# Attention scores in blocks of 32 keys: four matmuls of 32 columns where one of 125 stood

## The chip, the cores and the metric

The kernel runs on one NeuronCore of one Trainium2 chip; the other seven cores are idle. The core has engines with instruction streams of their own: PE (TensorE, matrix multiply; PEld is its weight load), ACT (ScalarE), DVE (VectorE), POOL (GpSimd) and SP, which here only issues DMAs. They meet through semaphores. The metric is device time in microseconds (us) of one execution, and less is better. The kernel before takes 2458.41 us (median of three runs, 2457.47 to 2459.47).

## The reference

The input is 8 waveforms of 120000 samples. Each is cut into 1500 frames of 80 samples, and then (biases and shapes cut):

```python
h = einsum('bfr,hr->bfh', x, W) + b          # 8 x 1500 x 256
h = gelu(layernorm(h) * ln_gamma + ln_beta)
n = layernorm(h)                             # 16 heads of 16 columns each
scores = einsum('bhqd,bhkd->bhqk', Q, K) / 4 # Q, K, V from n
attn = softmax(scores, axis=-1)              # 1500 x 1500 for each head and batch
h = h + einsum('bhqk,bhkd->bhqd', attn, V) @ Wo.T + bo
h = h + ffn(layernorm(h))
```

In the last line each of 16 experts takes 8 // 16 = 0 tokens of an axis of 8, so that `ffn` comes down to a layernorm with a scale and an offset per column. Nearly all the work is in the scores and their softmax: 8 x 16 x 1500 x 1500 exponentials, 288 million.

## The kernel before

**Tiling.** A batch is one waveform. Its 1500 tokens are 12 tiles of 125 (`T`), or 3 chunks of 500 (`QC`). Its 16 heads are 4 groups of 4. A unit is one group of heads and one chunk of 500 queries; there are 12 units in a batch and 96 in the kernel. A unit takes all 1500 keys. An item is one head and one tile of 125 keys against the 500 queries: a score block of 125 x 500. A unit has 48 items, done in 8 rounds of 6, so the kernel has 96 x 8 = 768 rounds and 4608 items.

**Score matmuls.** Queries and keys are kept as two halves of 16 bits each, so that one head has 64 rows (`KR`) to sum over. Even heads lie on partitions 0 to 63, odd heads on 64 to 127. One item is one matmul on line 829: 64 rows, 125 columns of weights (the keys), 500 moving columns (the queries). Items come in pairs, an even and an odd head, and `scores(n, first, 2, ...)` issues one pair: it fills two of PSUM's banks 0 to 5, and only its last matmul raises the semaphore `s_sc`.

**The round.** Program order on PE in a round is: pair one (banks 4 and 5), pair two (banks 0 and 1), pair three (banks 2 and 3), then the attends, then the pieces beside. Each pair first waits (`s_ex`) until ACT has emptied the banks it writes. ACT has three exponentials in a round, each over 2 banks (125 x 1000): line 486 for banks 0 and 1, line 489 for banks 2 and 3, line 494 for banks 4 and 5. So pair one of a round feeds line 494 of the same round, while pairs two and three feed lines 486 and 489 of the next. The three pairs of banks are all the buffering there is between the two engines.

**Attends.** `attend` (line 853) multiplies the exponentials of one tile of keys with V: four program matmuls, one for each head, each 125 rows by 32 columns of weights and 500 moving columns in f32. Every f32 matmul is two in the trace, so one attend is 8 there. Even rounds have one attend and odd rounds two; the second of an odd round waits for line 494 of its own round. The results gather in bank 6 or 7, and a column of ones in V gives the softmax's sums.

**Pieces.** Work of the next batch, and the output of the last, is cut into pieces (`tok`, `turn`, `qk`, `val`, `norm`, `flag`, `out`), placed by the table `PLAN` into rounds, usually one a round. Their matmuls (lines 774, 790, 799, 819, 806) already work in blocks of 32 columns, made by `blocks(n)`; `turn` (line 783) transposes with 128 columns. The table is the same in both kernels. Once a batch, in unit 2, ACT leaves the exponentials for a GELU.

**The second pass.** `exact_max` is a path with exact row maxima that runs only if a bound on the scores fails. It doesn't run on this input.

Of the kernel before, what the change touches and what calls it, by code (L numbers as in the profile page):

```python
# [5 lines left out]
def audio_tower(nc, x, tok_wT, tok_b, tok_g, tok_be, wqT, bq, wkT, bk, wvT, bv, woT, bo, ln_g, ln_b, out):  # L6
# [5 lines left out]
    NT, T = x.shape[2], x.shape[3]  # L12
# [3 lines left out]
    QC = 500  # L16
# [121 lines left out]
    with ExitStack() as ctx:  # L138
        def sb(name, shape, dt=f32):
            return ctx.enter_context(nc.sbuf_tensor(name, shape, dt))  # L140

        ident = sb("ident", [128, 128])
        ones = sb("ones", [128, 128])
# [17 lines left out]
        QA = sb("QA", [128, 2, 2, S], f16)  # L161
        KA = sb("KA", [128, 2, 2, S], f16)
# [8 lines left out]
        diag = sb("diag", [T, HG, QC])  # L171
# [15 lines left out]
        PS = ctx.enter_context(nc.psum_tensor("PS", [128, 8, 512], f32))  # L187
# [577 lines left out]
        def _(pe):  # L765

            def blocks(n):
                return [(lo, min(lo + 32, n)) for lo in range(0, n, 32)]
# [54 lines left out]
            def scores(n, first, count, exact_max):  # L823
                g, c = (n % NU) // NC, n % NC
                G = n // NC
                for m in range(first, first + count):
                    t, h, bank = m // HG, m % HG, m % 6
                    rows = slice(64 * (h % 2), 64 * (h % 2) + 64)
                    last = pe.matmul(PS[0:T, bank, 0:QC], KA[rows, G % 2, h // 2, t * T:(t + 1) * T],  # L829
                                     QA[rows, G % 2, h // 2, c * QC:(c + 1) * QC], start=True, stop=not exact_max)  # L830
                    if exact_max:
                        last = pe.matmul(PS[0:T, bank, 0:QC], ones[0:T, 0:T], diag[:, h, :], start=False, stop=True)
                last.then_inc(s_sc, 1)

            def row_scores(n):
# [43 lines left out]
            def unit(b, u, exact_max):  # L879
                n = b * NU + u  # L880
                R0, bank, used = PER * n, 7 - n % 2, UNIT_USES[n]
                if exact_max or n == 0:
                    if u % NC == 0:
                        pe.wait_ge(s_ld, at(s_ld, 64 * (n // NC + 1)))
                    if n > 0:
                        pe.wait_ge(s_ex, at(s_ex, 3 * R0))
                    if exact_max:
                        row_scores(n)
                    scores(n, 0, 2, exact_max)
                    scores(n, 2, 2, exact_max)  # L890
                for r in range(PER):
                    R = R0 + r
                    if R > 0:
                        pe.wait_ge(s_ex, at(s_ex, 3 * R))
                    scores(n, 6 * r + 4, 2, exact_max)
                    pe.wait_ge(s_ex, at(s_ex, 3 * R + 1))
                    if r == PER - 1 and not exact_max and n + 1 < B * NU and (u + 1) % NC == 0:
                        pe.wait_ge(s_ld, at(s_ld, 64 * ((n + 1) // NC + 1)))
                    for j in range(2):
                        if j:  # L900
                            pe.wait_ge(s_ex, at(s_ex, 3 * R + 2))
                        if r < PER - 1:
                            scores(n, 6 * r + 6 + 2 * j, 2, exact_max)
                        elif not exact_max and n + 1 < B * NU:
                            scores(n + 1, 2 * j, 2, False)
                    q = r // 2
                    if r == 0:
                        pe.wait_ge(s_free, at(s_free, used))
                        if n > 1:
                            pe.wait_ge(s_ov, at(s_ov, n - 1))  # L910
                    if r % 2 == 0:
                        attend(n, 3 * q)
                    else:
                        attend(n, 3 * q + 1)
                        pe.wait_ge(s_ex, at(s_ex, 3 * R + 3))
                        attend(n, 3 * q + 2)
                    used = beside(b, u, r, bank, used)
# [86 lines left out]
```

## Time and profile before

| | |
|---|---|
| time, median of 3 | 2458.41 us |
| profiled execution, its own time | 2458.36 us |
| its span, first to last instruction | 2456.6 us |
| mean granted TensorE clock, share of 2.4 GHz | 0.971 |
| PE busy, matmuls | 2237.6 us, 19500 |
| ACT busy | 2155.3 us, 2332 instructions |
| DVE busy | 920.3 us |
| POOL busy | 371.5 us |
| DMA | 133.62 MB, 54 GB/s |

A busy share adds up the time in which at least one instruction of the engine is under way. Matmuls overlap, and the profile models their ends, so what matters for PE is the time from the start of one matmul to the start of the next. The exponentials on ACT overlap as well: each is on the books for about 1.01 us while the next starts 0.88 to 0.90 us after it.

### The profile page before, as it was taken

How to read it: one execution, taken by the hardware profiler on the slowest of the kernel's cores; microseconds unless marked ns; L12 is line 12 of the kernel's file. 1: busy time of each engine (PE TensorE's matmuls, PEld its weight loads, DVE VectorE, ACT ScalarE, POOL GpSimd, SP SyncE). 2: the span in 40 equal slices, each digit the busy share in tenths (PEclk: the TensorE clock that was granted, in tenths of full speed). 3: DMA queues.
4: the chain of work that ended last, by engine and by line, in shares of the span. 5: the costliest groups of instructions: out<-in, count | busy, mean ns of one | idle time of the engine just before them, and what ended most of it. 6: DMA issues, size and time to landing. Idle time of an engine off the chain costs nothing.

```text
span 2456.6 us, 47924 instructions
## 1 busy us (share of the span) xinstructions
PE 2237.6 (91%) x19500; PEld 669.8 (27%) x19500; DVE 920.3 (37%) x2075; ACT 2155.3 (88%) x2332; POOL 371.5 (15%) x495
## 2 busy tenths in 40 slices
PE   4589999999999999999999999999999999998892
PEld 1222223222232223222232222322222222222221
DVE  7442235432354334532345233542335332330114
ACT  0098999989999899998999899998999989999991
POOL 2211102211021111210112110211112110110002
PEclk7799999999999999999999999999999999999996
DMA  2311221222112222212212221222222122111101
GB/s 71 107 37 40 66 67 41 57 66 65 50 40 66 64 66 49 57 48 58 74 40 52 70 66 40 50 62 60 69 54 50 41 65 67 47 44 39 33 6 32
DMA packets 109922, 133.62 MB, mean 54 GB/s; under 512 B 32263, under 2 KB 89670, under 8 KB 109694
## 3 DMA queue, kind: packets, MB, share of 16 engines
q1 hardware_dynamic: 107158, 128.64, 20.8%
q8 instruction: 156, 2.56, 0.4%
q10 hardware_dynamic: 2536, 1.83, 0.3%
q14 instruction: 72, 0.59, 0.1%
HBM read 55.16 MB, written 61.44 MB: 47 GB/s over the span
## 4 chain that ended last, share of the span: by engine, by line
issue 47%; PE 27%; ACT 10%; POOL 8%; DVE 3%; POOLq 1%; DMA 1%; SPq 1%; DVEq 0%; ACTq 0%
PE PS L853 12%; PE PS L829 8%; PE PS L790 5%; ACT prob L489 4%; ACT prob L486 4%; POOL sq L380 2%; POOL Y L388 2%; ACT prob L494 2%; POOL rs L390 2%; POOLq L389 1%; PE PS L799 1%; PE PS L774 1%; DVE z L550 1%; DVE HL L568 1%; POOL rs L367 1%
## 5 line engine op out<-in xcount | busy, mean ns | idle before, releaser
L853 PE MATMUL PS<-prob,Vst 125*32 125x500 f32 x9216 | 1131.4, 593 | 0.2 <-ACT prob L489 0.2
L494 ACT ACTIVATE prob<-PS 125x1000 f32<-125x1000 f32 x768 | 776.4, 1011 | 135.9 <-PE PS L829 134.6
L829 PE MATMUL PS<-QA,KA 64*125 64x500 f16 x4608 | 769.0, 406 | 84.5 <-ACT prob L489 45.7
L486 ACT ACTIVATE prob<-PS 125x1000 f32<-125x1000 f32 x768 | 775.3, 1010 | 80.4 <-PE PS L829 80.3
L489 ACT ACTIVATE prob<-PS 125x1000 f32<-125x1000 f32 x768 | 784.4, 1021 | 0.0
L829 PEld LDWEIGHTS PS<-QA,KA 64*125 64x125 f16 x4608 | 255.9, 131 | 861.6 <-ACT prob L486 413.6
L853 PEld LDWEIGHTS PS<-prob,Vst 125*32 125x32 f32 x9216 | 219.6, 108 | 424.6 <-issue 242.5
L566 DVE TENSOR_SCALAR HL<-PS,b_qk 128x500 f16<-128x500 f32 x96 | 70.9, 739 | 504.1 <-PE PS L790 427.7
L790 PE MATMUL PS<-zT,w_qk 128*32 128x500 f32 x1536 | 197.4, 596 | 8.9 <-DVE Osb L611 7.6
L380 POOL TENSOR_TENSOR sq<-HL 128x2000 bf16<-128x2000 f16 x24 | 84.5, 3522 | 752.4 <-DVE HL L568 752.4
L611 DVE COPY Osb<-PS 128x500 f32<-128x500 f32 x96 | 65.0, 677 | 257.5 <-PE PS L853 257.5
L819 PE MATMUL PS<-w_o,oT 128*32 128x256 f32 (+1 forms) x1536 | 102.5, 388 | 36.7 <-DMA oT<-On 22.2
L799 PE MATMUL PS<-w_v,zT 128*32 128x256 f32 (+1 forms) x1536 | 104.2, 394 | 21.6 <-DVE Vst L573 20.9
L385 POOL TENSOR_SCALAR rs<-mv 125x1 f32<-125x1 f32 x96 | 26.1, 272 | 595.6 <-DVE mv L633 595.0
L623 DVE TENSOR_TENSOR On<-Den,Osb 128x500 f32<-128x500 f32 x96 | 103.7, 1080 | 7.9 <-issue 0.9
L629 DVE TENSOR_TENSOR Hs<-Hs,PS 125x256 f32<-125x256 f32 x96 | 39.6, 412 | 166.4 <-PE PS L819 166.4
L790 PEld LDWEIGHTS PS<-zT,w_qk 128*32 128x32 f32 x1536 | 48.1, 113 | 129.9 <-issue 100.8
L819 PEld LDWEIGHTS PS<-w_o,oT 128*32 128x32 f32 (+1 forms) x1536 | 46.2, 111 | 113.3 <-issue 36.2
L642 DVE SCALAR_TENSOR_TENSOR Y<-Hs,rs,Y 125x256 f32<-125x256 f32 x96 | 73.2, 763 | 7.2
L517 DVE BATCH_NORM_STATS2 st<-PS 125x6 f32<-125x256 f32 x96 | 36.5, 422 | 102.8 <-PE PS L774 102.8
L799 PEld LDWEIGHTS PS<-w_v,zT 128*32 128x32 f32 (+1 forms) x1536 | 47.2, 111 | 99.3 <-issue 38.7
L568 DVE SCALAR_TENSOR_TENSOR HL<-PS,b_qk,HL 128x500 f16<-128x500 f32 x96 | 70.9, 739 | 7.9 <-issue 0.9
(79 smaller groups left out, 955.0 us busy)
## 6 DMA issues: line engine op xcount, KB each, us to landing
qk_halves_scratch<-HL SPq DMA_DIRECT2D x384, 125.0 KB
QA<-qk_halves_scratch SPq DMA_DIRECT2D x64, 375.0 KB, 5.0
KA<-qk_halves_scratch SPq DMA_DIRECT2D x64, 375.0 KB, 7.2
oT<-On SPq DMA_DIRECT2D x384, 31.2 KB, 2.0
out<-Y SPq DMA_DIRECT2D x24, 500.0 KB
X<-in_x SPq DMA_DIRECT2D x8, 468.8 KB, 7.9
thin<-Osb SPq DMA_DIRECT2D x96, 7.8 KB
Den<-thin SPq DMA_DIRECT2D x96, 7.8 KB
```

Of the source, the lines that this page charges most:

```text
L380: pool.tensor_tensor(sq[:, :, :], HL[:, :, 0, :], HL[:, :, 0, :], ALU.mult).then_inc(s_sq, 1)
L486: act.activation(prob[0:T, 6 * p:6 * p + 2, :], PS[0:T, 0:2, 0:QC], ACT.Exp, scale=scl)\
L489: act.activation(prob[0:T, 6 * p + 2:6 * p + 4, :], PS[0:T, 2:4, 0:QC], ACT.Exp, scale=scl)\
L494: act.activation(prob[0:T, 6 * p + 4:6 * p + 6, :], PS[0:T, 4:6, 0:QC], ACT.Exp, scale=scl)\
L568: dve.scalar_tensor_tensor(out=HL[:, i % 4, 1, :], in0=PS[:, bank, 0:QC], scalar=bias, in1=HL[:, i % 4, 0, :], op0=ALU.add, op1=ALU.subtra ...
L623: dve.tensor_tensor(On[:, :], Den[:, :], Osb[:, :], ALU.mult).then_inc(s_on, 1)
L642: dve.scalar_tensor_tensor(out=y, in0=h, scalar=rs3[:, n % 2:n % 2 + 1], in1=y, op0=ALU.mult, op1=ALU.add).then_inc(s_y, 1)
L790: ins = pe.matmul(PS[lo:hi, bank, 0:QC], w_qk[:, c, w, m * 128 + lo:m * 128 + hi], zT[:, c, :], start=(c == 0), stop=(c == KC - 1))
L799: last = pe.matmul(PS[lo:hi, bank, 0:D], zT[:, c, t + lo:t + hi], w_v[:, c, :], start=(c == 0), stop=(c == KC - 1))
L819: last = pe.matmul(PS[lo:hi, bank, 0:D], oT[:, m, e * T + lo:e * T + hi], w_o[:, m, :], start=(m == 0), stop=(m == KC - 1))
L829: last = pe.matmul(PS[0:T, bank, 0:QC], KA[rows, G % 2, h // 2, t * T:(t + 1) * T], QA[rows, G % 2, h // 2, c * QC:(c + 1) * QC], start=Tr ...
L853: last = pe.matmul(PS[lo:lo + 2 * HD, 6 + n % 2, 0:QC], Vst[:, b % 2, t, g * HG + j, :], prob[0:T, (HG * t + j) % 12, :], start=(t == 0), ...
```

## The change

Where an item was one matmul with 125 columns of weights, it is four: blocks of 32, 32, 32 and 29 keys. Each block writes its own 32 partitions of the same PSUM bank, and all four read the same 500 queries. The same is done in the path that doesn't run here. The pair's last matmul, which raises the semaphore, is now the fourth block of the odd head. `blocks` is the helper that the other matmuls use already.

```python
def blocks(n):
    return [(lo, min(lo + 32, n)) for lo in range(0, n, 32)]
```

```diff
                     t, h, bank = m // HG, m % HG, m % 6
                     rows = slice(64 * (h % 2), 64 * (h % 2) + 64)
-                    last = pe.matmul(PS[0:T, bank, 0:QC], KA[rows, G % 2, h // 2, t * T:(t + 1) * T],
-                                     QA[rows, G % 2, h // 2, c * QC:(c + 1) * QC], start=True, stop=not exact_max)
+                    for lo, hi in blocks(T):
+                        last = pe.matmul(PS[lo:hi, bank, 0:QC], KA[rows, G % 2, h // 2, t * T + lo:t * T + hi],
+                                         QA[rows, G % 2, h // 2, c * QC:(c + 1) * QC], start=True, stop=not exact_max)
                     if exact_max:
-                        last = pe.matmul(PS[0:T, bank, 0:QC], ones[0:T, 0:T], diag[:, h, :], start=False, stop=True)
+                        for lo, hi in blocks(T):
+                            last = pe.matmul(PS[lo:hi, bank, 0:QC], ones[0:T, lo:hi], diag[:, h, :],
+                                             start=False, stop=True)
                 last.then_inc(s_sc, 1)
```

On PE, in the middle of a batch, the end of an odd round and a whole even round with a `qk` piece read like this before (QA and KA are queries and keys, prob the exponentials, Vst is V, zT and w_qk belong to the piece):

```order
L853 MATMUL PS<-prob,Vst 32x500 x8
L790 MATMUL PS<-zT,w_qk 32x500 x4
L829 MATMUL PS<-QA,KA 125x500 x6
L853 MATMUL PS<-prob,Vst 32x500 x4
L790 MATMUL PS<-zT,w_qk 32x500 x4
```

The same even round, from its second item on, is this in the changed kernel:

```order
L830 MATMUL PS<-QA,KA 32x500 x3
L830 MATMUL PS<-QA,KA 29x500
L830 MATMUL PS<-QA,KA 32x500 x3
L830 MATMUL PS<-QA,KA 29x500
L830 MATMUL PS<-QA,KA 32x500 x3
L830 MATMUL PS<-QA,KA 29x500
L830 MATMUL PS<-QA,KA 32x500 x3
L830 MATMUL PS<-QA,KA 29x500
L830 MATMUL PS<-QA,KA 32x500 x3
L830 MATMUL PS<-QA,KA 29x500
L856 MATMUL PS<-prob,Vst 32x500 x4
L790 MATMUL PS<-zT,w_qk 32x500 x4
```

Six matmuls have become 24, and nothing has moved past anything else: the order of pairs, attends and pieces is unchanged, and so are all other engines.

## Rows read from the trace of the kernel before

**Rows 1.** The page: busy time and instructions, and the clock in 40 slices.
```profile
PE 2237.6 (91%) x19500; PEld 669.8 (27%) x19500; DVE 920.3 (37%) x2075; ACT 2155.3 (88%) x2332; POOL 371.5 (15%) x495
...
PEclk7799999999999999999999999999999999999996
...
q8 instruction: 156, 2.56, 0.4%
```

**Rows 2.** Waits of ACT and PE, 130 to 2290 us: total us, times, longest.
```profile
ACT prob L494 <- PE PS L829: 132.3, 160, 4.1
...
PE PS L829 <- ACT prob L489: 37.5, 95, 0.5
```

**Rows 3.** Timeline of ACT, 1204.4 to 1211: start us, us, what it ran.
```profile
1204.51 1.01 ACT L489 ACTIVATE prob<-PS 125x1000 f32<-125x1000 f32 x1
...
1206.30 1.02 ACT L486 ACTIVATE prob<-PS 125x1000 f32<-125x1000 f32 x1
1207.18 1.03 ACT L489 ACTIVATE prob<-PS 125x1000 f32<-125x1000 f32 x1
1208.21 1.00 ACT L494 ACTIVATE prob<-PS 125x1000 f32<-125x1000 f32 x1
...
1210.00 1.01 ACT L489 ACTIVATE prob<-PS 125x1000 f32<-125x1000 f32 x1
```

**Rows 4.** Timeline of PE from 1202.26: one row for each group of matmuls.
```profile
1202.26 0.92 PE L829 MATMUL PS<-QA,KA 64*125 64x500 f16 x6
...
1205.93 1.04 PE L853 MATMUL PS<-prob,Vst 125*32 125x500 f32 x8
1206.79 1.02 PE L790 MATMUL PS<-zT,w_qk 128*32 128x500 f32 x8
1207.75 0.94 PE L829 MATMUL PS<-QA,KA 64*125 64x500 f16 x6
```

**Rows 5.** Timeline of PE in windows under 0.1 us: pairs and sets of four.
```profile
1202.26 0.42 PE L829 MATMUL PS<-QA,KA 64*125 64x500 f16 x2
1202.52 0.66 PE L829 MATMUL PS<-QA,KA 64*125 64x500 f16 x4
1205.58 0.42 PE L829 MATMUL PS<-QA,KA 64*125 64x500 f16 x2
1205.93 0.63 PE L853 MATMUL PS<-prob,Vst 125*32 125x500 f32 x4
1206.37 0.60 PE L853 MATMUL PS<-prob,Vst 125*32 125x500 f32 x4
...
1204.40 0.60 PE L853 MATMUL PS<-prob,Vst 125*32 125x500 f32 x4
1204.93 0.42 PE L829 MATMUL PS<-QA,KA 64*125 64x500 f16 x2
```

**Rows 6.** Durations of lines 829, 853 and 806: ns, least, median and most.
```profile
L829 PEld LDWEIGHTS PS<-QA,KA x4608: 128/129/228, 116.3 to 2401.4; 64*125 64x125 f16 x192
L829 PE MATMUL PS<-QA,KA x4608: 368/421/675, 116.4 to 2401.4; 64*125 64x500 f16 x192
...
L853 PE MATMUL PS<-prob,Vst x9216: 579/582/1041, 119.6 to 2403.4; 125*32 125x500 f32 x197
...
L806 PEld LDWEIGHTS PS<-sq,head_sel x96: 92/97/102, 67.1 to 2097.2; 128*32 128x32 bf16 x96
L806 PE MATMUL PS<-sq,head_sel x96: 371/376/600, 67.1 to 2097.6; 128*32 128x500 bf16 x96
```

**Rows 7.** Timeline of PE: one norm piece after a wait, four matmuls of 16 bits.
```profile
100.72 0.40 PE L806 MATMUL PS<-sq,head_sel 128*32 128x500 bf16 x4 [2.15 <-POOL sq L380]
```

**Rows 8.** Timeline of PE: the last transpose of a turn, and the pair behind it.
```profile
1183.12 0.48 PE L783 MATMUL PS<-ident,z 125*128 125x125 f32 x3
1183.33 0.27 PE L783 MATMUL PS<-ident,z 125*128 125x125 f32 x1
...
1183.53 0.43 PE L829 MATMUL PS<-QA,KA 64*125 64x500 f16 x2
```

## The prediction, made before the changed kernel ran

> **What bounds the kernel now.** I read the page's busy shares first, then the waits, then short timelines of ACT and PE side by side. PE is busy for 91% of the span and ACT for 88% [rows 1]: two engines near full, so the question is how they are tied. In the waits, PE waits for ACT in some places (pair three for line 489) and ACT for PE in others (line 494 for a pair) [rows 2]. Neither is simply the bound; they take turns in a loop.
>
> The timelines show the loop. Exponentials start 0.88 to 0.90 us apart, except at 1208.21, which comes 1.03 us after the one at 1207.18 [rows 3]: ACT stood about 0.14 us. Follow that back. Line 494 at 1208.21 needed pair one, which started at 1207.75, so 0.46 us from a pair's start to its exponential. Pair one stood behind a `qk` piece (1206.79), and that behind an attend (1205.93) [rows 4]. The attend stood behind pair three at 1205.58 [rows 5], and pair three had waited for the exponential of line 489 that ran from 1204.51 to 1205.52 [rows 3]. The chain from one line 489 to the line 494 four places on is
>
> 1.07 (exponential and its signal) + 0.35 (pair three to attend) + 0.86 (attend) + 0.96 (piece) + 0.46 (pair one to line 494) = 3.70 us,
>
> where ACT alone would need 4 x 0.885 = 3.54 us. From line 494 the next line 489 follows two places on, 1.79 us later (1208.21 to 1210.00), and the loop closes: 3.70 + 1.79 = 5.49 us for two rounds. The PE rows say the same: pair one at 1202.26 and at 1207.75, 5.49 us apart [rows 4]. ACT's floor for two rounds is 6 x 0.885 = 5.31 us. Where pieces are heavier, PE never waits and its own sum is the period. So in both regimes a nanosecond on PE's path between pairs and attends counts, down to ACT's floor, and 384 such double rounds make the kernel. What lies outside (start, the GELU once a batch, the end) has no part in the change.
>
> **The change, part by part.** 4608 score matmuls become 18432, and as many weight loads. All that counts is what one pair costs PE: two matmuls before, eight now.
>
> *Streaming.* A matmul occupies its part of the array for its 500 moving columns. Two matmuls of a pair, on the two halves of the rows, start together: two end within 0.42 us, and the median of a single one is 421 ns [rows 5, 6]. The second pair starts at 1202.52, 0.26 us after the first, and the third joins within 0.24 us [rows 5]. Four matmuls of 32 columns side by side also start together: four of line 806 take 0.40 us in all, where one has 371 to 376 ns [rows 6, 7]. So neither splitting rows in two nor columns in four costs streaming time. No row shows both splits at once. Bounds: eight start together (0 added), or the two heads go one after the other (0.21 us added to a pair: 500 columns at 2.4 GHz). I take 0, since both splits alone are free.
>
> The Trainium skill, "TensorEngine Tiling (Array Packing)", Tiling Modes, lists 64 rows by 32 columns as a mode with eight tiles that load and multiply independently; no row here has that mode, so this is only cited.
>
> *Weight load.* The first pair after a wait, or behind a change of shape, can't load ahead. Its matmuls show 421 ns against a least of 368 [rows 6], and its distance to the next is 0.26 where 0.21 would be the stream: 0.05 us of load laid open for 125 columns. The load instruction itself is 129 ns for 125 columns and 97 for 32 [rows 6], so 32 ns less; scaled by the columns, 0.052 x 32/125 leaves 13 ns open, so 39 less. I take a gain of 37 ns for each open load. Bounds: 0 (the loads of eight blocks queue up) and 52.
>
> *Spread.* Eight matmuls don't start in the same instant. Four of 16 bits take 0.40 us, of which one has 376 ns and the open load 13 [rows 6, 7]: some 11 ns for three steps, 3 to 4 ns each. Two score matmuls take 0.42, where one has 421 ns [rows 5, 6]: a few ns at most. Sets of f32 spread wider, 0.60 for four with a median of 582 ns [rows 5, 6], 18 to 20 ns for three steps. At 3.3 ns a step eight matmuls spread over 23 ns, 20 more than a pair now; at 6.7 ns, the pace of f32, 47, so 44 more. I take 3.3, as the operands have 16 bits. The pair's signal and the switch to the attends wait for the last.
>
> *The switch of shape.* From the last set of an attend to the next pair takes 0.53 us (1204.40 to 1204.93), where set to set takes 0.44 with an open load (1205.93 to 1206.37) [rows 5] and 0.42 without (1206.37 to 1206.79) [rows 4, 5]. So 0.09 us beyond spread and stream. It isn't only the columns: from the last transpose, with 128 columns and all rows, to a pair, with 125 columns and 64 rows, takes 0.20 us (1183.33 to 1183.53), where transposes follow at 0.11 (three take 0.48, one 0.27) [rows 8]. A change of rows alone costs about as much. In the changed kernel pairs and attends share the column shape and still differ in rows (64 and 125), so I keep 0.09 at both ends of the scores.
>
> The Trainium skill, "TensorEngine Tiling (Array Packing)", Key Properties, says that changing the tiling mode drains the engine. By that rule the switch stays, and the trace agrees with its 0.09 us.
>
> *Issue and instruction fetch.* PE gets 27648 more instructions beside 39000. Its instructions come in 156 packets, 2.56 MB in the whole run, 0.4% of the DMA engines [rows 1]; 1.77 MB more is nothing to 133 MB. I cost it at nothing; if PE's queue ran dry it would show as issue gaps of up to about a microsecond at each of some 110 more packets, 110 us at worst.
>
> *The sum.* Each chain passes two pairs with open loads (pair three, pair one) and two spreads: 2 x (-37 + 20) = -34 ns. A round in which PE never waits has one open load and one spread before the attends: -37 + 20 = -17, and two of them -34. Either way 34 ns for a double round, and 5.49 - 0.034 = 5.456 stays above ACT's 5.31. 384 x 0.034 = 13 us. Some rounds have slack or wait for DVE, which a faster PE doesn't help; I take off a tenth. Forecast: 2458.36 - 12 = 2446.4 us for the profiled execution, which is within 0.1 us of the median (2458.41), so 2446. Its own range goes from both loads at -52 with the small spread (384 x 2 x 0.032 = 25, 2434) to a load gain of 25 (2455).
>
> **Rivals.**
>
> *The spread eats the load.* With the pace of f32, 2 x (-37 + 44) = +14 ns a double round: 384 x 0.014 = +5 us, 2464. With no gain in the load and the small spread, 2 x 20: +15 us, 2474. With both against it, 2 x 44: +34 us, 2492. For it: f32 sets do spread so [rows 5], and eight loads have to pass seven waiting matmuls where four pass three. Against it: four matmuls of 16 bits spread less [rows 7]. It ends on the slower side when the spread of a pair grows by more than its open load shrinks, 37 ns. In the middle it is no change.
>
> *The two heads take turns.* If eight can't run at once, a pair takes 0.42 us instead of 0.21. Each chain has two pairs: 2 x 0.21 - 0.034 = +0.39 us, 148 us, 2606. With pair two in the way as well, where PE never waits, 6 x 0.21 = 1.26 a double round, 480 us, 2940. For it: no row has both splits. Against it: each is free alone.
>
> *The switch falls away.* If only the column shape drained the array, four switches of 0.09 us would go: 0.36 for a double round, of which ACT's floor leaves 5.49 - 5.31 = 0.18 in the light rounds. 384 x 0.18 = 69 us, 2390. For it: attends and pieces with 32 columns follow one another at the stream's pace (1205.93 to 1206.79 for two sets [rows 4]). Against it: rows 8.
>
> *Issue.* If the sequencer can't hand out the 16 instructions of a pair as fast as the four of today, the spread grows. With as much for each step as four matmuls have in all, 24 ns (0.40 less 0.376 [rows 6, 7]), eight spread over 7 x 24 = 168, 165 more than now: 2 x (165 - 37) = +0.26 us a double round, 98 us, 2556. Against it: those four start within that time together. The Trainium skill, "TensorE: Matmul & The Clock Gate", in Part 1, gives a floor of about 25 ns from start to start of small matmuls; across the parts of the array the trace contradicts it [rows 7].
>
> **Chances.** The forecast 0.54. The spread eats the load 0.28, most of it between 2454 and 2480. The heads take turns 0.04, the switch falls away 0.07, issue or fetch 0.07. A measurement can tell 0.2%, 5 us, so "same" is 2453.5 to 2463.3. Faster: 0.50 of the forecast's 0.54 and the 0.07, 0.57. Same: the rest of it, 0.04, and 0.14 of the second case, 0.18. Slower: 0.25. The range 2430 to 2482 holds the forecast and most of the second case and leaves out the last three.
>
> **What the profile after would show.** Line 830 with 18432 matmuls, in sets of eight that start within 25 ns. Open loads: the common matmul behind a wait some 13 ns above the least, where it is 53 now. Pair three to attend 0.34 us, attend to pair one unchanged at 0.53. Double rounds of 5.45 to 5.46 us. ACT's idle time before line 494 some 12 us below the 132.3 of rows 2, each exponential still about 1.01 us. The clock keeps its 9s. Wrong would be: sets of four 0.2 us apart (heads take turns), a pair to exponential time above 0.46 (spread), 0.44 from attend to pair (no switch), or gaps with no releaser on PE (fetch).

## The result, and the profile after

The changed kernel takes 2454.66 us (median of 20 runs) against 2457.69 for the kernel before: ratio 0.9985, with a 95% interval of 0.9978 to 0.9992. One run of each kernel was far slower (4097 and 11536 us), and the ratio is taken without them. That is 3 to 4 us faster, where 12 were forecast. The sign held, and so did the chain that the forecast followed, but not the size: two thirds of the gain are missing.

The page of the changed kernel, beside [rows 1]:

```profile
span 2453.0 us, 75572 instructions
PE 2220.3 (91%) x33324; PEld 613.4 (25%) x33324; DVE 920.1 (38%) x2075; ACT 2153.5 (88%) x2332; POOL 370.5 (15%) x495
...
PEclk7799999999999999999999999999999999999996
...
q8 instruction: 264, 4.33, 0.7%
```

13824 matmuls more, and PE's busy time is 17 us less. A busy time that adds up modelled lengths says little here. ACT's waits for PE between 130 and 2290 us, beside [rows 2]:

```profile
ACT prob L494 <- PE PS L830: 129.7, 153, 4.1
```

132.3 before, so 2.6 us less, which is about what the total shows. Durations of line 830, beside [rows 6]:

```profile
L830 PEld LDWEIGHTS PS<-QA,KA x18432: 87/89/148, 116.3 to 2397.7; 64*32 64x32 f16 x150, 64*29 64x29 f16 x49
L830 PE MATMUL PS<-QA,KA x18432: 367/382/622, 116.3 to 2397.7; 64*32 64x500 f16 x152, 64*29 64x500 f16 x47
```

The common matmul fell from 421 ns to 382. Above the least of its row that is 53 ns before and 15 now, the load that lies open: the load term as forecast. Now one chain in short windows of the timeline (start, length, what, how many): pair three, the attend behind it, then pair one and line 494, which stood waiting for it:

```profile
1081.74 0.40 PE L830 MATMUL PS<-QA,KA 64*32 64x500 f16 x8
1082.07 0.63 PE L856 MATMUL PS<-prob,Vst 125*32 125x500 f32 x4
...
1083.89 0.40 PE L830 MATMUL PS<-QA,KA 64*32 64x500 f16 x8
1083.33 1.04 ACT L489 ACTIVATE prob<-PS 125x1000 f32<-125x1000 f32 x1
1084.36 1.00 ACT L494 ACTIVATE prob<-PS 125x1000 f32<-125x1000 f32 x1
```

All eight matmuls of a pair lie within 0.40 us: the two splits together cost no streaming. Pair three to attend is 0.33 us, 0.35 before [rows 4, 5], as forecast. But pair one to line 494 is 0.47 to 0.48 us, 0.46 to 0.47 before [rows 3, 4], where the forecast's 17 ns less would be 0.45, and more than 0.46 was to be a sign of being wrong. The rows round these to 10 ns; the medians over all rounds, from the trace's start times in ns, are the two distances on which everything below rests:

| median, ns | before | changed |
|---|---|---|
| first to last matmul of a pair | 3 | 23 |
| pair one to pair two, its load open | 262 | 222 |
| **pair three to attend** | 354 | 334 |
| **pair one to line 494**, where ACT waited | 467 | 477 |
| the second bold row less the first: what only ACT's start sees | 113 | 143 |
| pair one to the rise of its semaphore, where ACT waited | 444 | 455 |
| two rounds | 5511 | 5503 |

The spread of 23 ns and the load gain of 40 are the forecast's to a few ns. The signal to ACT is 30 ns later beyond both. The trace also holds the moment at which `s_sc` rises (the last row but one). ACT starts 22 or 23 ns behind it in both kernels, so the lateness is in the semaphore's rise and not in ACT.

### The profile page after: what moved, and what is told of

The parts are those of the page before. It is cut to its first block, busy times and chain, and to the rows that moved or that the text cites. A ratio compares the mean times of both kernels' runs of the same rounds, so it can differ in the third digit from the quotient of the medians.

```text
span 2453.0 us, 75572 instructions
## 1 busy us (share of the span) xinstructions
PE 2220.3 (91%) x33324; PEld 613.4 (25%) x33324; DVE 920.1 (38%) x2075; ACT 2153.5 (88%) x2332; POOL 370.5 (15%) x495
## 4 chain that ended last, share of the span: by engine, by line
issue 49%; PE 21%; ACT 14%; POOL 8%; DVE 3%; DMA 2%; POOLq 1%; SPq 1%; DVEq 0%; ACTq 0%
PE PS L856 9%; ACT prob L489 6%; PE PS L830 6%; ACT prob L486 5%; PE PS L790 4%; POOL sq L380 2%; POOL Y L388 2%; ACT prob L494 2%; POOL rs L390 2%; DMA qk_halves_scratch<-HL 1%; SPq L246 1%; DVE HL L568 1%; DVE HL L566 1%; POOLq L389 1%; DVE z L550 1%
## 5 line engine op out<-in xcount | busy, mean ns | idle before, releaser
L830 PE MATMUL PS<-QA,KA 64*32 64x500 f16 (+1 forms) x18432 | 751.9, 381 | 97.5 <-ACT prob L489 48.8
L830 PEld LDWEIGHTS PS<-QA,KA 64*32 64x32 f16 (+1 forms) x18432 | 200.5, 90 | 907.3 <-ACT prob L486 416.2
L573 DVE TENSOR_TENSOR Vst<-PS,b_v 125x256 f32<-125x256 f32 x96 | 40.1, 421 | 88.5 <-PE PS L799 88.5
```

Source lines behind the costliest of these rows:

```text
L830: last = pe.matmul(PS[lo:hi, bank, 0:QC], KA[rows, G % 2, h // 2, t * T + lo:t * T + hi], QA[rows, G % 2, h // 2, c * QC:(c + 1) * QC], st ...
```

## The experiments

The theory after the trace, called the tail below: the semaphore that starts ACT is raised about 5 ns later for each matmul that ends with the last one. Its rival: the double rounds are bound by something else, and the chain's nanoseconds don't count. A narrower one: the lateness belongs to the shape with 32 columns, not to the number.

### Blocks of 64 keys

```diff
-                    for lo, hi in blocks(T):
+                    for lo, hi in ((0, 64), (64, T)):
```

> Blocks of 64 and 61 keys: four matmuls for each pair instead of two (before) or eight (changed). Tail theory: the signal of a pair comes about 4.8 ns later for each further matmul that ends with it, beside the spread of the starts (3.3 ns each) and less the open load saved (25 ns for 61 columns). From a pair's first matmul to line 494: 467 - 25 + 7 + 10 = 459 ns (467 before, 477 changed). Pair three to attend: 354 - 25 + 7 = 336 ns. Together -26 ns a double round, 384 times: 10 us below the kernel before, about 2448. Rival, the open load never reached the signal and the spread does by half: 470 ns and 336 ns, -15 ns, about 2452. Rival, the light double rounds are bound by something other than this chain: about 2455 as with the changed kernel.

Measured: 2448.14 us (5 runs) against 2458.12, ratio 0.9959 (0.9945 to 0.9972). The two distances are 457 and 334 ns, 459 and 336 expected by the tail. The same chain in this kernel:

```profile
1075.71 0.41 PE L830 MATMUL PS<-QA,KA 64*64 64x500 f16 x4
1076.04 0.63 PE L856 MATMUL PS<-prob,Vst 125*32 125x500 f32 x4
...
1077.86 0.41 PE L830 MATMUL PS<-QA,KA 64*64 64x500 f16 x4
1078.32 1.00 ACT L494 ACTIVATE prob<-PS 125x1000 f32<-125x1000 f32 x1
```

Pair three to attend is the same 0.33 us as with blocks of 32 (less load gained, less spread paid), and pair one to line 494 is 0.46. Here 30 ns of a chain are saved instead of 10, and the time falls by 10 us instead of 3.7 (0.0041 and 0.0015 of 2458). That rejects the rival that other things bind the light rounds. It is also the kernel that beats both: the intervals of the two ratios don't overlap, though the two kernels were not measured side by side.

### Blocks in pairs two and three, or in pair one alone

```diff
-                    for lo, hi in blocks(T):
+                    for lo, hi in (((0, T),) if m // 2 % 3 == 2 else blocks(T)):
```

(the other kernel has the two choices exchanged)

> Pair one of each round whole (125 columns), pairs two and three in blocks of 32; so the column shape changes between pair one and pair two at the same 64 rows. Tail theory and additive chain: pair one to line 494 back at 467 ns, pair three to attend 334 ns, so the short waits of ACT before line 494 go from 156 ns (before) and 151 (changed) to about 136. Pair one to pair two takes 262 before and 223 changed; if a change of columns alone drains, it takes about 0.31 us here. Where PE never waits that costs some 40 to 50 ns a round, hidden in rounds in which pair three waits for ACT. Total 2450 to 2458. Rival, bound elsewhere: short waits stay at 151 to 156. Rival, a change of columns alone doesn't drain: 0.21 to 0.26 us from pair one to two and a total near 2450.

Measured: 2456.07 us (11 runs), ratio 0.9998 (0.9989 to 1.0007): no change. Pair one to line 494 is back at 466 ns. Pair one to pair two takes 355 ns instead of 262, so a change of columns alone, at the same 64 rows, costs 93 ns:

```profile
1205.35 0.42 PE L830 MATMUL PS<-QA,KA 64*125 64x500 f16 x2
1205.70 0.60 PE L830 MATMUL PS<-QA,KA 64*32 64x500 f16 x13
```

The second row starts 0.35 us after the first (it holds pair two and the start of pair three, since the window cuts it). Behind the turns of unit 3, where the whole wait of two rounds falls on one exponential, ACT's wait went from 156 ns to 136, as expected: the 20 ns of pair three arrive whole. In most other rounds pair three now starts late behind the extra switch of shape, since its own wait for ACT is too short to cover it, and the waits are divided otherwise (141 and none before, 77 and 40 in unit 9). The total stands still because gains and losses meet. A batch has 48 double rounds; taken from line 494 to line 494 (medians over the six middle batches), 32 of these places are 20 ns faster, but six are 25 to 48 ns slower, one is 192 slower, and one, of which more below, 234.

> The other way round: pair one in blocks of 32, pairs two and three whole. Tail theory: pair one to line 494 477 ns, pair three to attend 354, short waits of ACT 156 + 10 = 166 ns, and a switch more in each round where PE never waits: 2460 to 2468. Rival, bound elsewhere: short waits at 151 to 156 and a total near 2457.

Measured: 2465.85 us (6 runs), ratio 1.0033 (1.0021 to 1.0045), within what was expected. Pair one to line 494 477 ns, as in the changed kernel, so the lateness goes with the pair that is in blocks: the semaphore rises 454 ns after pair one's start here, and 444 in the kernel with blocks in pairs two and three. The wait behind the turns is 174 and not 166: the switch isn't wholly hidden, which the expectation had wrong.

### The same matmuls cut along the queries

```diff
-                    last = pe.matmul(PS[0:T, bank, 0:QC], KA[rows, G % 2, h // 2, t * T:(t + 1) * T],
-                                     QA[rows, G % 2, h // 2, c * QC:(c + 1) * QC], start=True, stop=not exact_max)
+                    for q0, q1 in ((0, QC // 2), (QC // 2, QC)):
+                        last = pe.matmul(PS[0:T, bank, q0:q1], KA[rows, G % 2, h // 2, t * T:(t + 1) * T],
+                                         QA[rows, G % 2, h // 2, c * QC + q0:c * QC + q1],
+                                         start=True, stop=not exact_max)
```

> Whole 125 keys, the 500 queries of each item in two matmuls of 250: four matmuls for each pair, of which only two end together. Tail theory by matmuls that end together: pair one to line 494 467 + 3 to 5 ns, short waits 160, total 1 to 3 us above the kernel before. Rival, the tail is by the number of instructions since the last signal: 467 + 10 + 5 = 482 ns, total about +6 us. If loading the same weights again is not hidden under 104 ns of stream, pair to pair grows by about 50 ns and the total by 20 us or more.

Measured: 2462.37 us (11 runs), ratio 1.0017 (1.0007 to 1.0026).

```profile
1083.00 0.43 PE L830 MATMUL PS<-QA,KA 64*125 64x250 f16 x4
1083.36 0.63 PE L854 MATMUL PS<-prob,Vst 125*32 125x500 f32 x4
...
1085.18 0.33 PE L830 MATMUL PS<-QA,KA 64*125 64x250 f16 x2
1085.66 1.00 ACT L494 ACTIVATE prob<-PS 125x1000 f32<-125x1000 f32 x1
```

Pair three to attend is 362 ns, 8 more than before, and pair one to line 494 479, 12 more. The second is closer to the count of instructions (482) than to the count of those that end together (470 to 472). But most of it is seen by the attends too, so it is PE that is longer: the two heads now start 7 ns apart instead of 3. Of the tail proper, the difference of the two, 113 has become 117: 4 ns for two more instructions of which none ends together with the last pair, against 10 in the blocks of 64. So the number of instructions alone doesn't explain it, but a rest of 4 ns stays unexplained.

### Fewer matmuls in the same shape

Three kernels, one run each. The first leaves out the fourth block of every item, the second the odd heads with blocks of 32, the third the odd heads of the kernel before; their outputs lack those scores.

```diff
-                    for lo, hi in blocks(T):
+                    for lo, hi in blocks(T)[:3]:
```

```diff
+                    if h % 2:
+                        continue
                     rows = slice(64 * (h % 2), 64 * (h % 2) + 64)
```

> The changed kernel with the fourth block of every item (keys 96 to 124 of each tile) left out, so its scores aren't computed: six matmuls of 32 columns end together instead of eight. By the number of matmuls that end together (5 ns each): pair one to line 494 477 - 7 (spread) - 10 = 460 ns, pair three to attend 327 ns, the difference of the two 133 (143 with eight, 123 with four of 64, 113 with two). If the later signal belongs to the mode with 32 columns and not to the number: 470 ns, difference 143.

> The changed kernel with the odd heads' scores left out: four matmuls of 32 columns, on one half of the rows. By the number: pair one to line 494 477 - 13 - 20 = 444 ns, pair three to attend 321, difference 123. By the mode: 464 ns, difference 143.

> The kernel before with the odd heads' scores left out: one matmul of 125 columns for each pair. By the number: pair one to line 494 467 - 3 - 5 = 459 ns, pair three to attend 351, difference 108. If the signal's lateness isn't by the number of matmuls: 464 ns, difference 113.

Pair one and line 494 in the same round of each, six, four and one matmuls (the line numbers are those of each kernel):

```profile
1080.03 0.40 PE L830 MATMUL PS<-QA,KA 64*32 64x500 f16 x6
1080.48 1.00 ACT L494 ACTIVATE prob<-PS 125x1000 f32<-125x1000 f32 x1
```

```profile
1088.58 0.39 PE L832 MATMUL PS<-QA,KA 64*32 64x500 f16 x4
1089.03 1.00 ACT L494 ACTIVATE prob<-PS 125x1000 f32<-125x1000 f32 x1
```

```profile
1096.42 0.42 PE L831 MATMUL PS<-QA,KA 64*125 64x500 f16 x1
1096.88 1.00 ACT L494 ACTIVATE prob<-PS 125x1000 f32<-125x1000 f32 x1
```

0.45, 0.45 and 0.46 us from row to row. All kernels together, medians in ns:

| matmuls that end together | columns | pair one to line 494 | pair three to attend | difference |
|---|---|---|---|---|
| 1 (one head) | 125 | 458 | 351 | 107 |
| 2 (before) | 125 | 467 | 354 | 113 |
| 4 (one head) | 32 | 444 | 321 | 123 |
| 4 (blocks of 64) | 64 | 457 | 334 | 123 |
| 6 | 32 | 460 | 329 | 131 |
| 8 (changed) | 32 | 477 | 334 | 143 |

The difference rises by 5 ns a matmul, and two kernels with four have the same 123 with 32 columns on one half of the rows and 64 columns on both. So it is the number, not the shape. The semaphore's rise says the same without the attends: it comes 14, 19, 30, 30, 39 and 50 ns after the modelled end of the pair's last matmul (the rows of the table in order; 24 in the halves), and ACT starts 22 or 23 ns after the rise in every one of the kernels. The Trainium skill, "TensorE: Matmul & The Clock Gate", Why this matters for your kernels, has a fit of this kind for the tail of a set of tiles, with 4.7 ns for each tile; the slope here is (143 - 107) / 7 = 5.1, and the trace agrees.

The whole times of these three (2445.59, 2459.68 and 2486.26 us in one run each, against 2459.97) don't follow their chains in the last two. The mean granted clock was 0.962 in both (0.973 in the run of the kernel before beside them), and ACT's wait in the round behind the GELU grew from 0.2 us to between 1.6 and 2.4 in each batch after the first. That the lighter load of PE is why the clock was lower is not shown. They serve for the distances alone.

## Why the prediction was wrong

**What bounds the kernel: right.** The loop through pair three, attends, pair one and ACT was the right one. 20 ns off (blocks in pairs two and three) and 20 on (halves) moved the wait behind the turns of unit 3 from 156 ns to 136 and to 177, and 30 off (blocks of 64) to 128. Weighed with 384 double rounds, -10, -30 and +20 ns give -3.8, -11.5 and +7.7 us, against ratios that stand for -3.7, -10.1 and +4.2. The last is only half, and that isn't slack in the chain. Of the 48 double rounds of a batch, from line 494 to line 494, 41 are within 5 ns of -10 in the changed kernel, 39 within 5 ns of -30 with blocks of 64, and 39 within 5 ns of +20 in the halves, heavy ones among them.

What hides the rest is the clock. In unit 4 of every batch but the last, PE stands 3 us for DVE's `Vst`, and towards the end of that wait the granted clock falls from 2.4 to 1.2 GHz for 3.4 or 6.8 us, or not at all. The same 25 us of the second batch before and in the halves (window, its length, busy times, then the granted clock, DMA share and GB/s):

```profile
520.00:545.00 25.00, 21.61 (x181) 6.50 (x174) 9.29 (x22) 18.27 (x21) 7.13 (x4) 0.86 0.39 88
520.00:545.00 25.00, 21.59 (x244) 8.95 (x238) 10.34 (x24) 20.68 (x23) 7.14 (x4) 1.00 0.42 95
```

Each 3.4 us at the lower level costs some 1.3 us, and the traces of the halves and of the blocks of 64 have three fewer of them than the one before. Without the last four rounds of unit 4 in each batch, the three traces differ from the one before by -3.5, -10.6 and +7.3 us (the one with blocks of 64 is of its fastest run, 2444.04 us). So the factor of 384, less a tenth, holds each time.

**Streaming: right.** Eight matmuls over both splits start within 23 ns (the median; 25 at most among the third pairs). The rival in which the heads take turns is gone.

**Weight load: right.** 40 ns less for each open load, 37 taken.

**Spread: the start of it right, its use wrong.** This is the step that failed. The prediction took 3.3 ns a step, which is what came, and then let "the pair's signal and the switch to the attends wait for the last", both alike. For the attends that held (-20 ns measured, -17 forecast). For ACT it didn't: each of the six more matmuls delays the signal by another 5 ns, 30 in all, once in each chain. With that term the forecast's -34 ns for a double round would have been -4; the measured is -10 (-20 on the way to the attend, +10 on the way to line 494). 384 times the 24 ns between -34 and -10 is 9 us, about the whole error. The kernel before holds the price nowhere for PE to ACT, since there every pair has two matmuls; the bound should have been drawn from nought to something, and none was.

**The switch of shape: right.** Attend to pair one is 533 ns before and 532 now. The experiment with mixed pairs adds what was missing: a change of columns alone costs 93 ns. So either change alone costs what both cost together.

**Issue and fetch: right.** 108 more packets (264 against 156), 1.77 MB, and no gap that the profile puts down to them: line 830 waited 33.5 us in all where the profile says "issue", line 829 before 35.0.

**The rivals.** What came lies between the forecast and "the spread eats the load", by another way than its condition: the pace is not that of f32, but what a pair's signal loses (20 + 30 ns) is more than the open load gives (40). For pair one that rival's break-even is passed if the late signal counts as spread; pair three still gains, since there PE itself goes on and ACT isn't waiting for its signal. The stated range of 2430 to 2482 held the time, but its width came from other terms. The time also lies in the band that the forecast itself called "same" (2453.5 to 2463.3), to which it gave 0.18.

## What to carry to other kernels

Where a semaphore ends a set of matmuls that run side by side, price it from there to the waiting engine's start, and by the number in the set; the next matmul on PE doesn't see that delay. Narrow blocks shorten a weight load that lies open and lengthen the spread and the tail, so the best width is between: for this pair of 64 x 125 it is 64, of the three widths tried (125, 64 and 32). Before a difference of a few us is weighed against a chain, count the stretches at the lower clock in both traces. And leave blocks alone that would change the shape once more in a round, since that costs more than they give.

## What the runs showed that was not expected

- 5 ns for each matmul that ends with the signalling one (107 to 143 ns from one to eight), unseen by PE itself: the semaphore rises later, and ACT follows the rise by the same 22 or 23 ns.
- 93 ns for a change of columns at the same rows (355 against 262 ns), as much as rows alone or both.
- Once in nearly every batch a stretch at 1.2 GHz goes with a wait of 3 us on PE. Its length differs from batch to batch within one run (3.4 or 6.8 us, or none), and three such differences are worth as much as the whole change.
- Less work on PE made two kernels not faster (one head left out, 2459.68 and 2486.26 us against 2459.97, one run each): the mean granted clock was 0.962 against 0.973, with further stretches at 1.2 GHz of 3.4 to 13.7 us behind the GELU. Unit 2, where the GELU is, takes 19 and 24 us more than before over all batches.
